# Value products of two dense attention stages: one batch behind every second block of scores, or half a batch behind each block

## The reference

```python
# L0
attn = einsum('bnd,bmd->bnm', q * scale, k)
attn = attn + rel_h[..., :, None] + rel_w[..., None, :]
out  = softmax(attn, axis=-1) @ v                  # then a projection

# L3
attn = einsum('bhnd,bhmd->bhnm', q, k) * SCALE
attn = attn + einsum('bhnd,nmd->bhnm', q, tvk[iv] + thk[ih]) * SCALE
attn = softmax(attn, axis=-1)
out  = einsum('bhnm,bhmd->bhnd', attn, v)
out  = out + einsum('bhnm,nmd->bhnd', attn, tvv[iv] + thv[ih])
```

## Time and profile before

| what | value |
|---|---|
| median of three runs | 6802.88 us |
| the profiled execution | 6800.92 us |
| its span, from the first to the last instruction | 6799.0 us |
| mean granted TensorE clock, as a share of 2.4 GHz | 0.914 |
| PE busy, share of the span | 86% |
| ACT busy / DVE busy / POOL busy | 37% / 53% / 36% |
| L0B: first to last scores start | 464.9 to 1900.2 us |
| L3B: first to last scores start | 3991.8 to 5671.5 us |

### The profile page before, as it was taken

One profiled execution on the slowest core, in us unless ns is written; L12 is line 12 of the kernel. 1 busy time (PEld: TensorE's weight loads), 2 busy tenths in 40 slices (PEclk: granted clock), 3 DMA queues, 4 the chain that ended last, 5 costly groups with the idle time before them and its releaser, 6 DMA issues. The chain is left out here.

```text
span 6799.0 us, 129026 instructions
## 1 busy us (share of the span) xinstructions
PE 5839.6 (86%) x44140; PEld 3217.6 (47%) x44140; DVE 3615.3 (53%) x5453; ACT 2516.3 (37%) x3334; POOL 2457.0 (36%) x2361
## 2 busy tenths in 40 slices
PE   8579999999977976677668879999999997879996
PEld 6553333333353343457555733333333334868885
DVE  4247777777746964434554345555555553451212
ACT  2225555555522212222221235555555552112221
POOL 0045555555514941110000144454454451053023
PEclk9789999999998997778758989999999998979998
DMA  4853434333334210000001543333333335567665
GB/s 145 266 166 89 92 90 93 91 89 89 88 75 135 87 51 4 0 1 1 1 0 49 170 129 97 102 101 97 102 102 97 102 100 195 178 229 238 210 228 185
DMA packets 839800, 741.83 MB, mean 109 GB/s; under 512 B 514933, under 2 KB 722453, under 8 KB 828726
## 3 DMA queue, kind: packets, MB, share of 16 engines
q1 hardware_dynamic: 827062, 710.76, 35.9%
q0 software_dynamic: 12288, 25.18, 1.1%
HBM read 463.94 MB, written 278.00 MB: 109 GB/s over the span
## 5 line engine op out<-in xcount | busy, mean ns | idle before, releaser
L1176 DVE TENSOR_REDUCE L3B_nmax<-L3B_R 128x1 f32<-128x1024 f32 x768 | 939.1, 1224 | 711.8 <-PE L3B_R L1078 692.8
L1176 DVE TENSOR_REDUCE L0B_nmax<-L0B_R 128x1 f32<-128x1024 f32 x768 | 935.3, 1222 | 356.6 <-PE L0B_R L1078 342.7
L1162 ACT ACTIVATE L0B_PT<-L0B_R 128x1024 f32<-128x1024 f32 x768 | 785.3, 1023 | 695.0 <-PE L0B_R L1088 667.3
L1162 ACT ACTIVATE L3B_PT<-L3B_R 128x1024 f32<-128x1024 f32 x768 | 785.3, 1023 | 580.8 <-PE L3B_R L1088 539.9
L1088 PE MATMUL L0B_R<-L0B_QS,L0B_KS 64*128 64x512 bf16 (+1 forms) x6144 | 802.2, 381 | 70.0 <-issue 35.6
L1088 PE MATMUL L3B_R<-L3B_QS,L3B_KS 64*128 64x512 bf16 (+1 forms) x6144 | 793.6, 378 | 3.4 <-DVE L3B_nmax L1176 3.4
L1114 PE MATMUL L3B_O<-L3B_PT,L3B_VA 128*64 128x512 f32 x3072 | 743.8, 605 | 0.0
L1088 PEld LDWEIGHTS L3B_R<-L3B_QS,L3B_KS 64*128 64x128 bf16 (+1 forms) x6144 | 268.1, 94 | 589.3 <-DVE L3B_nmax L1176 308.0
L1088 PEld LDWEIGHTS L0B_R<-L0B_QS,L0B_KS 64*128 64x128 bf16 (+1 forms) x6144 | 258.6, 94 | 545.0 <-issue 214.1
L1109 PE MATMUL L0B_O<-L0B_PT,L0B_VA 128*32 128x256 f32 x6144 | 419.3, 389 | 4.9 <-issue 4.7
L2874 ACT ACTIVATE L3F_hidden<-L3F_H,L3F_weights 128x256 f32<-128x256 f32 x474 | 181.4, 481 | 489.4 <-PE L3F_H L2806 489.3
(11 more groups left out here) (408 smaller groups left out, 9086.5 us busy)
## 6 DMA issues: line engine op xcount, KB each, us to landing
L3F_weights<-in_L3F_w SPq DMA_DIRECT2D x79, 1251.0 KB, 5.8
scr_sumsL<-L3B_OT SPq DMA_DIRECT2D x96, 512.0 KB
L3C_sums<-scr_sumsL SPq DMA_DIRECT2D x96, 512.0 KB, 9.1
scr_rel<-L0R_terms SPq DMA_DIRECT2D x64, 384.0 KB
L0B_raw<-scr_rel SPq DMA_DIRECT2D x192, 128.0 KB
L3B_raw<-scr_rel SPq DMA_DIRECT2D x384, 64.0 KB
scr_parts<-L0B_qk_parts SPq DMA_DIRECT2D x96, 224.0 KB, 2.7
scr_parts<-L3B_qk_parts SPq DMA_DIRECT2D x96, 224.0 KB, 2.2
```

Of the source, the lines that this page charges most:

```text
L1162: nc.scalar.activation(PT[:, (8 * u + j) % NPT, :, :], score_pair(u, j), ACT.Exp).then_inc(s_exp, 1)
L1176: nc.vector.tensor_reduce(nmax[:, u % 2, 4 * t:4 * t + 1], pair.rearrange("p j n -> p (j n)"), AX, ALU.max, negate=True).then_inc(s_mx, 1)
```

## The change

`pv` gets an argument `side`. With side 0 it does its waits and the first half of the batch, with side 1 the second half and the raise of `s_pv`. Side 0 stays where the whole batch stood, behind M of an even block; side 1 stands behind M of the odd block after it. In L3 a half is one of the batch's two slots of probabilities (two matmuls of 512 columns), in L0 it is one half of the keys (four matmuls of 256 columns). Nothing else is moved or added; the numbers that others wait for are the same.

```diff
-            def pv(H, u, b):
-
-                pe.wait_ge(s_exp, 8 * H + 2 * b + 2)
-                if b == 0:
-                    pe.wait_ge(s_va, H + 1)
-                if b == 0 or (b == 2 and not L0):
-                    if L0:
-                        pos(pe, s_tr, H - 1)
-                    else:
-                        pos(pe, s_ot, 2 * H + b // 2 - 1)
-                pe.sem_inc(s_pew, 1)
+            def pv(H, u, b, side):
+
+                if side == 0:
+                    pe.wait_ge(s_exp, 8 * H + 2 * b + 2)
+                    if b == 0:
+                        pe.wait_ge(s_va, H + 1)
+                    if b == 0 or (b == 2 and not L0):
+                        if L0:
+                            pos(pe, s_tr, H - 1)
+                        else:
+                            pos(pe, s_ot, 2 * H + b // 2 - 1)
+                    pe.sem_inc(s_pew, 1)
                 if L0:
                     slot = (8 * u + 2 * b) % NPT
-                    for h in range(2):
+                    for h in (side,):
...
                 else:
-                    for slot, kp, f in batch_slots(b):
+                    for slot, kp, f in batch_slots(b)[side:side + 1]:
...
-                mm.then_inc(s_pv, 1)
+                if side == 1:
+                    mm.then_inc(s_pv, 1)
...
                         max_scores(max_pair(u, j), tile[0], tile[1], tile[3])
-                    if j % 2 == 0 and j >= 4:
-                        pv(H, u, (j - 4) // 2)
-                    if j % 2 == 0 and j < 4 and started:
-                        pv(H - 1, (u - 1) % NU, 2 + j // 2)
+                    if j >= 4:
+                        pv(H, u, (j - 4) // 2, j % 2)
+                    if j < 4 and started:
+                        pv(H - 1, (u - 1) % NU, 2 + j // 2, j % 2)
             groups(pe, steps)
             for b in (2, 3):
-                pv(HEADS - 1, NU - 1, b)
+                for side in range(2):
+                    pv(HEADS - 1, NU - 1, b, side)
```

## The result

The changed kernel takes 6966.86 us, the median of four runs (6959.78 to 6967.87), against 6801.54 us before (the three runs named ahead and a fourth): 1.0243 times as long, with a 95% interval of 1.0225 to 1.0261. Slower was forecast, and by the stall that was forecast, but 7014 us were given for it and a range that began at 6978; the measured time lies under it.

What follows compares the result with a forecast made beforehand. TensorE's chain and a wait for `exp` were taken to bound L3B, SyncE's queue L0B. 6800.9 us + 209 (L3B, +2.20 a unit from entries into V and copy stalls) + 4 (L0B) = 7014 us, range 6978 to 7055.

Steps and rivals of the forecast that it cites:

- the stall that was forecast: In L3B, M of block 4 and of the next unit's block 0 each start 1.04 us late, 2.08 a unit.
- What bounds the kernel: L3B: TensorE's chain plus one wait for `exp`, 17.56 us a unit; L0B: SyncE's queue, 15.02 us a unit.
- what the change removes: In L3B, M's waits for `exp` of the odd block go on all blocks: 0.97 us a unit.
- the wait of 0.20: In L3B before the change, the even block's M starts 0.20 us late, waiting for `exp` of the odd block.
- L0B: Stage without ScalarE copies: a unit stays at 15.0 to 15.1 us; 18 units pay 0.24 each, +4 us, bounds -10 to +23.
- What it adds to TensorE: Entries into V double at 0.26 us each; an L3B block takes 2.21 us, a unit 17.68, +11 us in the stage.
- The rule of the Trainium skill on weight loads: Weight loads overlap matmuls in flight only for other row groups, so V on all 128 rows can't be preloaded.
- The wait it adds, on ScalarE: In L3B, `copy_sums` waits for the later raise and holds `exp`, then M: 1.04 us twice a unit, bounds 0.94 to 1.14.
- The 0.15: Gap in us between two ScalarE operations, from 2.19 - 2 x 1.02, put between the copy's end and `exp`.
- The rivals: Alternatives: no copy stall 6816 us, 4%; free entries 6700, 2%, or with stall 6915, 3%; lower clock 7052, 8%.
- That `exp` passes the waiting copy: In L3B, `exp` of block 3 starts on its scores, so no stall: 6816 us, slower by 0.2%; chance 4%.
- The range: Forecast's spread -30 to +25 us, with the lower-clock case included: 6978 to 7055 us.

## Why the prediction was right and wrong

*What bounds the kernel*, *what the change removes*: right for L3B. It is TensorE's chain, and the wait of 0.20 is gone from all blocks that have no copy. Wrong for L0B, see below.

*What it adds to TensorE*: right to 0.01 us a block, 2.20 for 2.21. M to V is 0.31 where M hadn't waited; 0.32 was read from rows in which it had. Over eight blocks and 95 units that is 7.6 us less than forecast. The rule of the Trainium skill on weight loads that was weighed there ("TensorE: Matmul & The Clock Gate", Part 3, The mechanism) agrees with the trace at the new places as well: the half batch behind block 3 begins 0.31 behind M, and its last pair of passes begins 0.53 ahead of S, as that of a whole one did. No run isolates the rule from other costs of changing over.

*The wait it adds, on ScalarE*: right in its mechanism, its two places and everything up to the copy's start (2.32 behind S of block 3, as forecast), and mis-sized behind it. This is the step that failed. The prediction let `exp` start 0.73 behind the copy's start; it starts 0.48 behind. The stall is 0.80 and not 1.04, and the bounds of 0.94 to 1.14 didn't hold it. Twice a unit and 95 units: 45.6 us. With the 7.6 above, less 3 us by which M of block 0 is later still in some units, 2 us in L0B and 1 us in the other stages, that is the 47 us by which the time was missed.

The 0.15 was a misreading. It was the gap between two `exp` in a row that says 2.19 for two, and was taken for ScalarE's restart. But there the second `exp` waited for its own scores: S runs from 4306.58 for 1.03, so its last matmuls end at 4307.61, behind the first `exp`'s end at 4307.59, and no overlap was possible. A gap that a wait leaves says nothing of how fast the engine goes on. A row that does say it stood in the trace of the kernel before, near L3B's end, where both blocks' scores were ready:

```profile
5660.83 1.94 ACT L1162 ACTIVATE L3B_PT<-L3B_R 128x1024 f32<-128x1024 f32 x2 [1.77 <-PE L3B_R L1088]
```

1.94 for two of 1.02: the second starts 0.92 behind the first, 0.10 before the first ends. With -0.10 in place of +0.15 the forecast would have been 7014 - 190 x 0.25 = 6966 us; that this meets the measured time is partly luck, since the other terms that were off cancel to about 1 us.

*L0B*: +4 forecast, +6 in the profile, no difference in the times of the kernel with halves there alone. That the numbers lie close is luck, for the ground was wrong. The prediction took the mean unit of 15.02 us for a pace that SyncE's queue sets for every unit. In the trace of the kernel before, the six units ahead of a back edge and the step across it read

```profile
L1181 DVE STREAM_TRANSPOSE L0B_max_turned<-L0B_nmax x6: 211/211/213, 643.7 to 714.3; 128x32 f32<-128x32 f32 x6
L1181 DVE STREAM_TRANSPOSE L0B_max_turned<-L0B_nmax x2: 211/211/211, 714.3 to 732.3; 128x32 f32<-128x32 f32 x2
```

(714.3 - 643.7) / 5 = 14.1 us a unit, which is what the prediction's own sum gives for TensorE's chain, and 18.0 across the edge. Half of all units take 14.2 or less; the thirteen with an edge hold 63 of the 87 us by which the stage is longer than 95 times 14.1. The list of waits in L0B has the idle time there, before and after:

```profile
PE L0B_R L1088 <- issue: 35.6, 13, 3.6
...
PE L0B_R L1088 <- issue: 42.6, 14, 3.7
```

(One of the fourteen afterwards, of 0.4 us, is not an edge.) So what the change adds in L0B comes at the edge and not in the units in which SyncE's queue waits. With half batches everywhere half of all units take 14.1 us or less, against the 14.16 of the forecast.

*The rivals*: none came. That `exp` passes the waiting copy is refuted by the changed kernel itself, where its scores were ready at 4041.86 and it stood behind the copy until 4043.62; the strict order on ScalarE that the Trainium skill states ("TensorE: Matmul & The Clock Gate", "Architectural detail", engine queue depths), which no row of before could show, now has this one, and it agrees. The clock stayed at 1.00 in L3B through stalls of 0.8 us.

*The range*: its lower end, 6978, lies 36 us under the forecast, though the text works out 30 for it; the stall's own lower bound accounts for 190 x 0.10 = 19. Both bounds moved the copy and the restart by 0.1; the restart's sign was not among them.

## What to carry to other kernels

When work is moved behind a later point of one engine's program, look for who waits for its semaphore and what stands behind that wait in the other engine's order: here the moved half batch was 1.0 us of TensorE's time, and its raise cost 0.8 us twice a unit because a copy that could wait stood ahead of an `exp` that could not. The cure is to move the waiter back as well; splitting then cost and saved the same here, and paid only at the one block whose wait was longer than an entry into V costs.

Take the rate at which an engine goes from one instruction to the next from a row in which the second had nothing to wait for. Here the pair with a wait in it showed a gap of 0.15 us, and the pair with no wait an overlap of 0.10.

A mean over a stage is not a pace. L0B's 15.02 us a unit was about 14.1 in half of the units and 19 in thirteen; the starts of a row that stands once in a unit, read between two edges, show it.

## What the runs showed of the hardware that was not expected

ScalarE's operations overlap: a copy of 128 x 512 from PSUM lasts 0.58 us and holds the next operation for 0.48; an `exp` of 128 x 1024 lasts 1.02 and holds it for 0.92, where the next one's input was ready.

TensorE's branch back to the loop's start in L0B, every sixth unit, leaves it idle at "issue", for 3.05 us before and 3.61 us after the change at the first edge, and for a mean of 2.7 and 3.2 us over all thirteen. In L3B's loop of the same form the branch takes 0.21 us and no such gap follows. Whether the clock then falls to 1.2 GHz for some us did not go by the idle time alone: it held behind 3.05 us at one edge of the kernel before and fell behind 2.76 us at another.
